# Conditional weights folded into the projection weights, one product per batch and head group

## What is computed

```
h   = x @ W_cond[id] + b_cond[id]                # one 512x512 matrix per batch, picked by id
qkv = h @ w_qkv.T                                # 16 heads
s   = q k / sqrt(32) - slope_h * |i - j|,  causal
p   = 0.5 * (1 + s * rsqrt(1 + s*s));  p /= sum(p) + 1e-6
x1  = x + (p v) @ w_out.T
u   = x1 + relu(x1 @ W1[l] + b1[l]) @ W2[l] + b2[l];  z = layernorm(u) * gamma[l] + beta[l]
out = x1 + int8_matmul(quantize(z), weight_int8) * scales + bias   # one scale over all of z
```

## Time and profile before

| | |
|---|---|
| median of 3 runs | 2075.36 us (2074.72 to 2079.71) |
| the profiled execution | 2068.65 us, its span 2066.9 us |
| busy over the span | PE 1744.5, DVE 1743.6, ACT 1705.6, POOL 1692.9 us |
| weight loads (PEld) | 888.9 us |
| first pair starts on ACT | 90.76 us |
| last pair starts on ACT | 1939.22 us |

### The profile page before, as it was taken

How to read it: one execution, slowest core, us unless ns; L and a number is a source line. 1 busy time by engine, 2 the same in 40 slices (tenths; PEclk the granted TensorE clock), 3 DMA queues, 4 the chain that set the end, 5 groups by cost and what they waited for, 6 DMA issues and landing times.

```text
span 2066.9 us, 29449 instructions
## 1 busy us (share of the span) xinstructions
PE 1744.5 (84%) x10699; PEld 888.9 (43%) x10702; DVE 1743.6 (84%) x1730; ACT 1705.6 (83%) x1842; POOL 1692.9 (82%) x723
## 2 busy tenths in 40 slices
PE   5678988999989888888898889889798888988764
PEld 4464534454445534543443444334344434443331
DVE  4348888998999889979899999999798988998748
ACT  0038899899999999989999999899888998998652
POOL 3027889888988999889989999899788997898558
PEclk9899999999999999989999999999998998999989
DMA  6421021221122213322222221222212221211246
GB/s 193 150 57 48 18 62 32 81 74 38 33 61 54 60 33 89 89 83 59 84 78 72 54 63 49 63 68 53 51 46 68 53 73 44 59 56 52 77 163 208
DMA packets 143260, 147.17 MB, mean 71 GB/s; under 512 B 28012, under 2 KB 94572, under 8 KB 142700
## 3 DMA queue, kind: packets, MB, share of 16 engines
q1 hardware_dynamic: 143116, 145.29, 24.8%
HBM read 54.28 MB, written 30.93 MB: 41 GB/s over the span
## 4 chain that ended last, share of the span: by engine, by line
PE 31%; ACT 24%; DVE 20%; issue 10%; POOL 8%; SPq 3%; DMA 2%; DVEq 0%; POOLq 0%; ACTq 0%
ACT yb L822 9%; DVE gb L1161 8%; ACT gb L787 7%; ACT yb L824 7%; DVE gb L1228 7%; PE sc L1004 6%; PE ov L982 6%; PE dn L982 5%; POOL yb L748 4%; PE it L916 3%; SPq L498 3%; PE it L900 3%; PE it L896 3%; POOL oT L781 2%; PE it L927 2%
## 5 line engine op out<-in xcount | busy, mean ns | idle before, releaser
L748 POOL TENSOR_TENSOR yb<-yb 128x1024 f32<-128x1024 f32 x544 | 1496.3, 2762 | 286.2 <-DVE gb L1228 269.0
L1228 DVE TENSOR_TENSOR gb<-sc,yb 128x1024 f32<-128x1024 f32 x544 | 662.4, 1218 | 159.3 <-ACT yb L824 154.7
L1161 DVE TENSOR_TENSOR gb<-gb,yb 128x1024 f32<-128x1024 f32 x544 | 764.4, 1405 | 1.3 <-POOL yb L748 1.1
L822 ACT ACTIVATE yb<-sc 128x1024 f32<-128x1024 f32 x544 | 550.3, 1012 | 171.3 <-PE sc L1004 85.4
L1004 PE MATMUL sc<-qmv,kst 128*128 128x512 f32 (+3 forms) x1280 | 467.9, 449 | 181.3 <-DVE gb L1228 165.8
L824 ACT ACTIVATE yb<-yb 128x1024 f32<-128x1024 f32 x544 | 575.7, 1058 | 17.3
L787 ACT ACTIVATE gb<-gb 128x1024 f32<-128x1024 f32 x544 | 566.3, 1041 | 0.0
L1004 PEld LDWEIGHTS sc<-qmv,kst 128*128 128x128 f32 x1280 | 225.1, 199 | 488.6 <-DVE gb L1228 343.8
L982 PE MATMUL ov<-gb,vv 128*32 128x512 f32 (+3 forms) x2560 | 318.3, 580 | 22.2 <-DVE den L1177 15.7
L982 PE MATMUL dn<-gb,ones 128*32 128x512 f32 (+3 forms) x2560 | 305.8, 560 | 0.0
L896 PE MATMUL it<-hT,wT 128*128 128x512 f32 x496 | 238.2, 598 | 2.7 <-ACT area L799 1.2
(11 more groups left out here) (119 smaller groups left out, 1128.4 us busy)
## 6 DMA issues: line engine op xcount, KB each, us to landing
qmv<-stage SPq DMA_DIRECT2D x384, 64.0 KB
kst<-stage SPq DMA_DIRECT2D x384, 64.0 KB
area<-in_x_dram SPq DMA_DIRECT2D x58, 256.0 KB, 2.8
out_dram<-oT SPq DMA_DIRECT2D x32, 256.0 KB, 3.2
wT<-wT_d SPq DMA_DIRECT2D x7, 768.0 KB, 4.4
h_d<-area SPq DMA_DIRECT2D x16, 256.0 KB, 2.6
hT<-h_d SPq DMA_DIRECT2D x4, 1024.0 KB, 6.3
o_d<-oT SPq DMA_DIRECT2D x4, 1024.0 KB, 4.5
```

The costliest lines, as they stand in the source:

```text
L748: pool.tensor_tensor(y, y, y, ALU.mult).then_inc(s_y2, 1)
L822: act.activation(yview(n), sc[:, n % SLOTS], ACT.Square).then_inc(s_s2, 1)
L1161: dve.tensor_tensor(gview(n), gview(n), yview(n), ALU.add).then_inc(s_num, 1)
L1228: dve.tensor_tensor(gview(n), sc[:, n % SLOTS], yview(n), ALU.mult).then_inc(s_g, 1)
```

## The change

The conditional weights are multiplied into the projection weights: for each batch and head group one 512 x 384 matrix is made from three 512x128 blocks (jobs `fu`, three for a group) and its bias from three columns (job `fb`), and q, k and v are made from the transposed raw tokens. The jobs `h` and the buffer `xT` are gone. The bias of q and k is added where `stage` is written, that of v by `hand_out`: the sum over keys times the bias is added to `ov`. The transposes of `w_qkv` (`wt`), of `W_cond` (`ct`), `w_out` (`wo`) and the int8 weights (`w8`, with a cast `c8` on DVE) are jobs spread over the groups of batch 0, each with its own load through the two `xin` buffers (`c8` has its own), and most results go to DRAM through two buffers `hst`. The prologue keeps: `wt` 0 to 2, `xt` 0 to 3, `ct` 0 to 3, `fb`, `fu` 0 and 1, q0, k0, `xt` 4 to 7, `fu` 2. Its transposes are emptied by ACT. SOFT_EPS is added in `invert`, after the sums are copied.

```diff
-def cond_jobs(j, start=0, end=0):
-    xt = Job(("xt", j), [0.45], (), start, end)
-    return [xt, Job(("h", j), [0.86] * 4, (xt,), start, end)]
+def raw_jobs(what, tiles, start, end):
+    return [Job((what, j), [0.45], (), start, end + n) for n, j in enumerate(tiles)]
+def fused_jobs(b, hg, raws, start, end):
+    fb = Job(("fb", 4 * b + hg), [0.3], tuple(raws), start, end)
+    return [fb] + [Job(("fu", 3 * (4 * b + hg) + s), [0.86] * 4, tuple(raws[s:s + 1]) + (fb,), start, end + 2 * s) for s in range(3)]
...
-        wanted = [(("q", 1), 0, 0), (("k", 1), 0, 8), (("v", 1), 0, 13)] if opens else []
+        wanted = [(("q", 1), 0, 0), (("v", 0), 0, 3), (("k", 1), 0, 8), (("v", 1), 0, 13)] if opens else []
...
+    later = raw_jobs("wt", range(3, 6), 5, 18)
+    opening = Group(NC, [raw_jobs("xt", range(2 * TT, 3 * TT), 1, 4) + later + raw_jobs("xt", range(3 * TT, KB), 10, 22),
+                         fused_jobs(0, 1, later, 8, 32)], True, True, 0.9)
+    raw2, raw3 = raw_jobs("wt", range(6, 9), 1, 12), raw_jobs("wt", range(9, 12), 1, 36)
+    fused2, fused3 = fused_jobs(0, 2, raw2, 1, 30), fused_jobs(0, 3, raw3, 1, 60)
+    for job in raw3:
+        job.after += (fused2[0], fused2[1 + job.name[1] % 3])
+    spare_a = Group(NC, [raw2 + raw_jobs("wo", range(0, 2), 1, 20) + raw3 + raw_jobs("wo", range(2, KC), 1, 50) +
+                         raw_jobs("xt", range(0, 4), 1, 60), fused2 + fused3], True, slack=0.6)
+    turned = raw_jobs("ct", range(KC), 1, 20)
+    fused4, fused5 = fused_jobs(1, 0, turned, 1, 40), fused_jobs(1, 1, [], 1, 60)
+    eights = [job for n in range(KC) for c8 in [Job(("c8", n), [], (), 4, 60)]
+              for job in (c8, Job(("w8", n), [0.45], (c8,), 4, 60))]
+    spare_b = Group(NC, [turned + raw_jobs("xt", range(4, 12), 1, 56), fused4 + fused5, eights], True, slack=0.6)
+    closing = Group(NC, [raw_jobs("xt", range(12, KB), 1, 24), fused_jobs(1, 2, [], 1, 40) + fused_jobs(1, 3, [], 1, 60)], True, slack=0.6)
...
+            sp.dma_start(wq_raw, wq_t[:, :, 0]).then_inc(s_raw[0], 16)
+            sp.dma_start(x_raw[0], x_t[0, 0:TT].rearrange("j p d -> p j d")).then_inc(s_raw[1], 16)
...
+            sp.dma_start(wc_raw, cond_w[bass.ds(cids[0], 1)].rearrange("a (k p) m -> p (a k) m", p=P)).then_inc(s_raw[2], 16)
+            cond_bias(0)
+            sp.dma_start(x_raw[1], x_t[0, TT:2 * TT].rearrange("j p d -> p j d")).then_inc(s_raw[3], 16)
...
             sp.wait_ge(s_zero, 2)
+            sp.wait_ge(s_evac, Setup.rank("q", 0))
             operand(0, 0, 0)
+            sp.wait_ge(s_evac, Setup.rank("k", 0))
             operand(1, 0, 0)
...
+                    elif what in RAW:
+                        r = raw_at[G, e[1].name]
+                        if r + 2 < len(raw_list):
+                            sp.wait_ge(s_item, base + item + 1)
+                            load_raw(r + 2)
+                    elif what == "w8" and c + 1 < KC:
+                        sp.wait_ge(s_w8f, c + 1)
+                        load_eight(c + 1)
+                    elif what == "fu" and c >= 3 * NG and c % 3 == 2 and c // 3 % NG < NG - 1:
                         sp.wait_ge(s_item, base + item + 1)
+                        load_plain(c // 3 % NG + 1)
...
-            act.wait_ge(s_wst, 48)
...
+            def fused(bank, j, blocks):
+                for blk in blocks:
+                    for k in range(KC):
+                        r = pe.matmul(bank[:, blk * P:(blk + 1) * P], wcT[:, k, blk * P:(blk + 1) * P], wst[:, j % 3, k, :],
+                                      start=(k == 0), stop=(k == KC - 1))
+            def fused_bias(bank):
+                for s in range(3):
+                    for k in range(KC):
+                        r = pe.matmul(bank[:, s:s + 1], wst[:, s, k, :], cbias[:, k:k + 1], start=(k == 0), stop=(k == KC - 1))
...
-                dve.tensor_copy(out_slice(hg, c), ov[:, :])
-                dve.tensor_scalar(den[:, :], dn[:, :], SOFT_EPS, None, ALU.add).then_inc(s_out, 1)
+            def hand_out(G, hg, c):
+                dve.tensor_copy(den[:, :], dn[:, :]).then_inc(s_dn, 1)
+                dve.wait_ge(s_dn, G * NC + c + 1)
+                dve.scalar_tensor_tensor(out=out_slice(hg, c), in0=den[:, :], scalar=bfs[:, G % 2, 2:3], in1=ov[:, :],
+                                         op0=ALU.mult, op1=ALU.add).then_inc(s_out, 1)
             def invert(G, c):
                 dve.wait_ge(s_den, 16 * (G * NC + c + 1))
+                dve.tensor_scalar(rec[:, :], rec[:, :], SOFT_EPS, None, ALU.add).then_inc(s_re, 1)
+                dve.wait_ge(s_re, G * NC + c + 1)
                 dve.reciprocal(rec[:, :], rec[:, :]).then_inc(s_rec, 1)
```

More of the change, by code:

```diff
@@ L137, in __init__ @@
         made = {}
+        others = [job for track in tracks for job in track]
         for job in others:
-            if job.name[0] == "h" and opens:
+            if job.name[0] == "xt" and opens:
                 made.setdefault(job.name[1] // TT, []).append(job)
@@ L225, in adaln_attn_ffn @@
     UNITS, PAIRS = len(plain.units), len(plain.pairs)
[L227 to L236, removed]
+    later = raw_jobs("wt", range(3, 6), 5, 18)
[13 more added lines that the diff above has]
+    closing = Group(NC, [raw_jobs("xt", range(12, KB), 1, 24), fused_jobs(1, 2, [], 1, 40) + fused_jobs(1, 3, [], 1, 60)], True, slack=0.6)
     def done_late(tiles, start):
-        return [job for j in tiles for job in after_jobs(j, start, PAIRS - 4, PAIRS - 2)]
+        return [[job for j in tiles if j % 2 == i for job in after_jobs(j, start, PAIRS - 4, PAIRS - 2)] for i in range(2)]
     joining = Group(NC, done_late(range(0, 5), 8), True, slack=0.7)
@@ L271, in adaln_attn_ffn @@
     REST, REST_DVE, REST_ACT = n
-    PRO_JOBS = woven(cond_jobs, range(TT))
+    raw_list, raw_at, kept, kept_at, fused_at, kept_before = [], {}, 0, {}, {}, {}
+    for b in range(B):
+        for hg, g in runs(b):
+            kept_before[b * NG + hg] = kept
+            for job in g.items:
+                if job.name[0] in RAW:
+                    raw_at[b * NG + hg, job.name] = len(raw_list)
+                    raw_list.append((job.name[0], job.name[1], batch_of(g, job.name)))
+                if job.name[0] in ("fu", "wo", "w8") or job.name[0] == "xt" and g is not opening:
+                    kept_at[b * NG + hg, job.name] = kept
+                    if job.name[0] == "fu":
+                        fused_at[job.name[1]] = kept
+                    kept += 1
     END_JOBS = woven(after_jobs, range(DONE, KB), KB - DONE)
@@ L357, in adaln_attn_ffn @@
         s_al = sem("s_al")
-        s_wst = sem("s_wst")
+        s_wst = [sem(f"s_wst_{i}") for i in range(3)]
+        s_wl = sem("s_wl")
+        s_bst = sem("s_bst")
+        s_raw8 = sem("s_raw8")
         s_wc = sem("s_wc")
@@ L661, in group @@
+                    if what == "n" and (g is joining if len(e[1].name) == 3 else g is closing):
                         keep_outputs(c)
@@ L664, in group @@
                     if g is closing and item == made_at:
-                        for a in range(2):
-                            sp.wait_ge(s_hst[a], 16 * 8)
+                        wait_kept(kept_at[G, ("xt", KB - 1)] + 1)
+                        sp.wait_ge(s_item, base + item + 1)
                         load_made(NC - 1)
+                    if g.has_next and item == load_at:
+                        sp.wait_ge(s_item, base + item + 1)
+                        load_fused(G + 1)
                     item += 1
@@ L829, in group @@
                         after(d, job, bases[0] + job.index, zs_before(d, job.name[1]))
+            for i, job in enumerate(Setup.items):
+                if Setup.ranks[i][0] == "act":
+                    what, j = job.name
+                    tok = slice(j * P, (j + 1) * P)
+                    dst = wst[:, j] if what == "wt" else (hT if what == "xt" else wcT)[:, :, tok]
+                    act.wait_ge(s_item, i + 1)
+                    act.activation(dst, it[:, i % BANKS].rearrange("p (k n) -> p k n", k=KC), ACT.Copy).then_inc(s_evac_act, 1)
             act.wait_ge(s_chain, 9)
-            act.wait_ge(s_wst, 48)
             for_groups(group)
```

362 lines of the change are left out of this document (198 added, 164 removed).

## The result

The changed kernel took 2102.21 us (median of 4 runs, 2086.35 to 2106.39), the kernel before 2075.56 us; the ratio is 1.0107 with a 95% interval of 1.0077 to 1.0137. So the change made the kernel about 1% slower. The forecast was 2016 us, range 1989 to 2044.

What follows compares the result with a forecast made beforehand. ACT sets the pace at 2.94 us a pair, with losses in prologue and `opening`. −35 − 47.5 + 12 + 5 + 3 + 2 + 1 = −59.5 from 2068.65 gives 2009, plus 6.7 to the median: 2016 us, range 1989 to 2044.

Steps and rivals of the forecast that it cites:

- prologue: Before the first pair: a shorter load and transpose chain brings the first L822 at 55.4 instead of 90.8 us, −35 us.
- `opening`: First group of 68 pairs: stalls while PE makes `h` go, 266.96 to 219.5 us, −47.5 us.
- the tail: Very end of the kernel: one more operation on 128x512, +1 us.
- Chunks of all groups: All groups: 31 inversions get one more small operation, `hand_out` two dependent operations; DVE work partly shows, +2 us (0 to 8).
- Slower: Rival, four groups: 41 raw loads through two `xin` buffers stand uncovered on PE, 115 us, giving 2131 us; chance 4%.
- Waits in these groups: `spare_a`, `spare_b`, `closing`: DVE waits three times for int8 loads, +5 us; `fb` of (1, 3) waits for a reload, +3.
- The +3 for `fb` of (1, 3): In `closing`: `fb` waits for the `wst` reload, issued only after the `fu` that frees it, +3 us (0 to 8).
- Spare groups and closing: `spare_a`, `spare_b`, `closing`: added PE and DVE work costs +4 us each, +12 in all.
- the slack named for it: In `spare_a`: PE's 18.4 us wait for DVE's L1228 could swallow the added work, falling below 12 us.

Runs made afterwards that it cites:

- the run with the later memset: POOL's second prologue memset (kst) waits for the end of DVE's chain, against the version with early int8 load and fb in three parts; 2039.0 us, ratio 0.9829.

## Why the prediction was wrong

Against the forecast, the profiled span is longer by 94.6 us. By the prediction's own terms: prologue −33.9 where −35 was forecast; `opening` −30.7 where −47.5; the two spare groups and `closing` +68.1 where 12 + 5 + 3 = 20; the four groups of batch 1 +26.6 where 2; the tail +4.9 where 1.

**The prologue and the start of the opening were right.** The first pair came at 56.86 us (forecast 55.4, 52 to 62), pair 1 5.8 us behind it (5 to 8). The conditional weights were there at 12.8 us (in the trace of the run with the later memset), forecast 12. One term was off: `fb` lay in PSUM until DVE's chain ended at 24.3, not 17.4, since L1245 stood beside both memsets. Most of that did not show, because the first of the two `fu` ran meanwhile: SP's first copy of q was issued at 33.6 instead of 30.4. The operand's DMAs (10.4 for 11.4 us) and the first scores (1.0 for 1.8) gave half of the rest back, which was luck. `opening` as a whole gained 30.7 instead of 47.5 us. Of the 16.8 us between, 12.3 go when the raw loads are left out (223.8 us). Another stall stands in every version of the changed kernel, and no run removes it: pair 41 takes 7 to 8 us, and PE stands 3.9 us there for the bias columns, which come back from DRAM (`bfs<-bf_d`).

**The step that failed is "Chunks of all groups".** I priced the 31 additional operations "below the 0.242 us of the reciprocal" and the whole term at +2 (0 to 8). They took 1.81 us each, 56.0 us, and cost 31 us (removed from the changed kernel) or 33 us (added to the kernel before). The nearest row by size was the wrong row: what mattered was that this is an addition whose operand and result lie in SBUF while POOL works; the reciprocal has the same operands and does not wait. L1134 of the kernel before stands at 4.65 us for the 1.2 us of its like, beside a memset of POOL; these rows were in its trace and I passed over them:

```profile
10.24 4.65 DVE L1134 TENSOR_SCALAR kst<-yb 16x2048 fp32r<-16x2048 int32 x1
10.31 3.50 POOL L720 MEMSET qmv<- 32x4096 f32 x1
```

The smaller half of the term: L1180 takes 0.74 us where L1086 took 0.68. The bias operand, priced at nothing, thus costs 0.06 us in each of 128 operations, 8 us of DVE, of which an unmeasured part shows. After SOFT_EPS is back, the four groups of batch 1 are together still 11.8 us longer than before. Up to 8.8 us of the difference between these two profiles is the choice of the execution (the one before lies 6.9 us below its median, this one 1.9 above); in the run without raw loads, with the same code in these groups, it is 6.1 us. This operand and the granted clock (0.931 against 0.947 over the kernel) are candidates for the rest, and it stays open.

**The rival "Slower" was real, and its chance too low.** I held against it that a load has two pairs, 6 us. Its own cost line named 8.5 us of operand copies in the same order, more than that. It did not strike all 41 raws, though: PE stood 6 to 8 us for one in each of `opening`, `spare_a` and `closing` and 3 us for one in `spare_b`. Leaving the loads out is worth 25 us, against the 115 us of the rival and 0 of the forecast. Their place in SP's order is shown for 8 of the 25 (the loads in the middle of an operand); whether the rest is place, the transfers themselves or SP's time for them was not separated.

**"Waits in these groups" was mis-sized.** DVE waited for the int8 tiles three times, as foreseen, but 14.7 us in all with 10.2 us the longest, where 0 to 3 each were priced. The price came from the landing, and in the longest wait that was 3.9 us; most of the rest was the operand ahead in SP's order. The one edit that removes it is worth 14 to 17 us, the term was +5. The +3 for `fb` of (1, 3) did not come: its reload was issued at 859.9 us, the job ran at 873.7, and PE shows no wait for it.

**"Spare groups and closing" held in PE's work, not in time.** PE came to 204.5 us in `spare_a` (forecast 203), but the group grew by 19.2 us where 4 was forecast. With SOFT_EPS back and the raw loads out it took 218.4 us, which is the +4. That the slack named for it pays for the work is not shown: PE's wait for DVE's product in `spare_a` should have fallen from 18.4 to below 12 us, and stood at 18.6 in the changed kernel and 16.4 without the raw loads. In the fastest version the three groups are still 23.6 us longer than before. And `fb`, rightly priced at 2.9 us of PE, was not asked for its price in the plan: 0.3. Planned at its price it is worth 9.4 us, cut up as well 15.5 us, part of which is the late pair 30 of `closing`. The Trainium skill, page "Perfetto Trace Analysis", section "Identifying the Most-Contended Engine", says to judge TensorE's headroom by the share of weight loads, among others, and not by matmul busy time. That share was 47% in `spare_a` before and 110.79 / 218.38 = 51% in the run without raw loads. If one reads that as room for the added work, the 3.9 us by which the group was still longer speak against it, but DVE had 7.6 us more to do there as well, so the run does not decide it.

The steps from the changed kernel to the fastest version, each measured on top of the one ahead, are 31 us (SOFT_EPS), 17 (int8 load), 15.5 (`fb`), 0 (memset) and 8 (raw loads): 71 us, to 2030.9. The forecast of 2016 lies another 15 us below, and what these are was not found.

## What to carry to other kernels

Price an added DVE operation by its kind, by where its operands lie and by what POOL does then, not by its size: with POOL busy nine tenths of a group, an addition within SBUF cost the rest of POOL's instruction (1.81 us on 128x16), while the same addition on the way out of PSUM took what the copy in its place took (0.68 us). The int8 cast within SBUF behaved alike, 1.96 us once beside POOL and 0.43 us three times without. It is not every operation within SBUF: reciprocals did not wait, nor did an addition on a single column, here in the changed kernel, which POOL accompanied in 29 of 32 cases:

```profile
L1220 DVE TENSOR_SCALAR vare<-mv 128x1 f32<-128x1 f32 x32 | 4.9, 154 | 1.1
```

So look for a row of the same kind and shape beside a busy POOL before pricing one.

When work is spread thin over a loaded schedule, ask of each new load what stands ahead of it in its issuing queue, and give the planner each new job's measured cost. A change may remove what it says (here 65 us, in the prologue and `opening`) and lose more by such small things (here 100 us, in the groups behind them).

## What the runs showed that was not expected

A tensor-scalar operation on 16 elements of each partition took 1.26 to 1.87 us beside POOL and 0.17 us without it, a reciprocal on the same ones 0.24 to 0.25 either way. Moving the start of all pairs 3.4 us ahead changed no time. And moving the raw loads to ACT's queue gained nothing on top of the early int8 load (2056.5 against 2054.3 us), while issuing them in the middle of an operand on SP gained 8 us.
